# Grouped attentions without a rough pass: scores kept in an SBUF ring, half-group maxima folded from them and added later

## The reference

```python
# 4 batches; 16 query heads, 4 key heads, head width 128; layer 1 also turns q and k by rotary tables
q = rms_norm(heads(x @ Wq), q_norm_w)
k = rms_norm(heads(kv_in @ Wk), k_norm_w)      # layer 1: kv_in = context and x, 1857 rows; layer 3: context, 1601
scores = einsum('bqhd,bkhd->bhqk', q, repeat(k, 4)) / sqrt(128)
out = einsum('bhqk,bkhd->bqhd', softmax(scores), repeat(v, 4)) @ Wo
x = x + out
```

## Time and profile before

| what | us |
| --- | --- |
| median of three runs (3725.1 to 3730.5) | 3728.4 |
| profiled execution, first to last instruction (its span; its own time stands nowhere else) | 3724.8 |
| first block and groups of the first grouped attention | 476.0 to 541.3 to 1753.9 |
| first block and groups of the second | 2487.0 to 2533.9 to 3597.5 |

### The profile page before, as it was taken

The page is one execution under the profiler, slowest core; times in us unless marked ns, Lnnn a source line. Parts: engine busy times, 40 slices in busy tenths (PEclk is TensorE's granted clock), DMA queues, the critical chain, the costliest instruction groups (busy, mean ns, idle before and its releaser), DMA issues. The chain is left out here.

```text
span 3724.8 us, 63821 instructions
## 1 busy us (share of the span) xinstructions
PE 3484.8 (94%) x23912; PEld 2986.2 (80%) x23912; DVE 2317.7 (62%) x4551; ACT 2244.6 (60%) x5208; POOL 863.9 (23%) x1082
## 2 busy tenths in 40 slices
PE   6859969999999999998899999888999999999999
PEld 5659958888888889987666665677989899889888
DVE  8976767766776676664777776435554555545434
ACT  3327736676676676665466666325666666666653
POOL 0022134222322222221121120212322322223214
PEclk8879979999999999999999999898999999999999
DMA  5216521100010010001100000121010110100001
GB/s 183 89 66 217 181 80 39 57 15 24 15 56 24 18 54 15 18 12 47 61 1 37 37 1 1 74 93 32 21 53 26 39 41 26 53 21 18 7 29 41
DMA packets 59186, 179.04 MB, mean 48 GB/s; under 512 B 6084, under 2 KB 27776, under 8 KB 53888
## 3 DMA queue, kind: packets, MB, share of 16 engines
q1 hardware_dynamic: 53024, 135.57, 10.6%
q0 software_dynamic: 3696, 37.68, 2.7%
q10 hardware_dynamic: 2160, 1.71, 0.2%
HBM read 147.14 MB, written 24.13 MB: 46 GB/s over the span
## 5 line engine op out<-in xcount | busy, mean ns | idle before, releaser
L1140 PE MATMUL ps<-a_v_rows,a_probs 128*128 128x129 f32 (+1 forms) x7168 | 943.3, 276 | 0.5 <-DVE a_o_rows L1508 0.5
L1140 PEld LDWEIGHTS ps<-a_v_rows,a_probs 128*128 128x128 f32 (+1 forms) x7168 | 894.5, 191 | 41.1 <-issue 5.1
L1252 ACT ACTIVATE a_probs<-ps 128x512 f32<-128x512 f32 (+1 forms) x896 | 535.6, 598 | 606.0 <-PE ps L1129 604.8
L1483 DVE TENSOR_REDUCE a_neg<-ps 128x1 f32<-128x1024 f32 (+2 forms) x512 | 539.7, 1055 | 397.0 <-PE ps L1104 396.4
L1262 ACT ACTIVATE ps<-a_negb 128x512 f32<-128x512 f32 (+1 forms) x892 | 536.7, 602 | 58.3 <-DVE a_negb L1498 30.3
L1324 POOL TENSOR_SCALAR a_diag<-ident,a_negmax 128x128 fp32r<-128x128 f32 x256 | 157.1, 614 | 1466.1 <-DVE a_negmax L1491 1464.5
L1125 PE MATMUL ps<-a_qt,a_kt 128*128 128x512 f32 (+1 forms) x896 | 428.0, 478 | 1.4 <-PEq L72 1.4
L1031 PE MATMUL ps<-a_wr,a_ct 128*128 128x256 f32 (+1 forms) x2496 | 362.9, 287 | 19.0 <-DMA a_ct<-ctx_lo 16.9
L1031 PEld LDWEIGHTS ps<-a_wr,a_ct 128*128 128x128 f32 (+1 forms) x2496 | 336.4, 188 | 44.7 <-issue 15.7
L1129 PE MATMUL ps<-a_qt,a_kt 128*128 128x512 f32 (+1 forms) x896 | 354.9, 396 | 0.0
L1127 PE MATMUL ps<-a_qt,a_kt 128*128 128x512 f32 (+1 forms) x896 | 354.0, 395 | 0.0
(11 more groups left out here) (469 smaller groups left out, 5992.5 us busy)
## 6 DMA issues: line engine op xcount, KB each, us to landing
a_wf<-in_a_wq SPq DMA_DIRECT2D x32, 512.0 KB, 3.6
a_wf<-in_a_wo SPq DMA_DIRECT2D x32, 512.0 KB, 3.6
a_ct<-ctx_hi SPq DMA_DIRECT2D x8, 1090.0 KB, 7.9
a_ct<-ctx_lo SPq DMA_DIRECT2D x8, 1090.0 KB, 10.2
f_we<-in_f_experts SPq DMA_DIRECT2D x8, 1088.0 KB, 8.8
a_wf<-in_a_wkv SPq DMA_DIRECT2D x32, 256.0 KB, 2.7
ctx_hi<-a_ct SPq DMA_DIRECT2D x4, 1602.0 KB, 5.4
ctx_lo<-a_ct SPq DMA_DIRECT2D x4, 1602.0 KB, 9.3
```

Source lines behind the costliest of these rows:

```text
L1140: ins = pe.matmul(m.ps[:, 6 + i // 2, (i % 2) * 256:(i % 2) * 256 + VW], probs[0:r, n % 3, i * P:(i + 1) * P], v_rows[g % 2][0:r, t, :], s ...
L1252: act.activation(probs[0:r, n % 3, :], m.ps[0:r, 4 + n % 2, :], ACT.Exp)\
L1483: ins = dve.tensor_reduce(neg2[:, j, r % 2:r % 2 + 1], flat2(m.ps[:, rough_at(task):rough_at(task) + 2, :])[:, 0:e - a0], AX.X, ALU.max, n ...
```

## The change

The rough pass is gone (R in all its parts, with L1104, L1483, L1491, L1324), and the seeds are gone. Now:

- `scores` start their own accumulation, in four banks (0, 1, 4, 5) instead of two.
- ACT copies each score tile from PSUM to a slot of an SBUF ring (`keep`; 20 slots in a1, 18 in a3), where before it seeded.
- DVE folds it into the half-group's running maximum `peak` (`highest`; 128x512, one operand in SBUF, one in PSUM; none for a half's first tile).
- After a half's last tile, task MX: PE transposes `peak` (4 matmuls), DVE reduces to `negmax`, POOL makes four diagonals at once; then NB as before, one turn later.
- POOL adds `negb` to each ring slot (`shift`), KT + 2 turns after the scores. In a3 every fourth tile is added by DVE, and so is every second tile of the very last half in both.
- ACT takes the exponential in the slot, KT + 3 turns after the scores, and PE's `values` read the slot in that same turn. The list of turns is one group longer, for what still runs after the last scores.
- One key and one query buffer: the next group's are written behind the scores that last read them. One weight buffer `wf` in place of three. x is read and updated where it is kept (`m.x`); XC and the DMAs of x are gone.

The core of the diff:

```diff
-        "R8 GA14", "R9 RA6 GA15", "R10 RA7 RA8", "XC0 RA9 R11", "RS0 R12", "R13", "R14", "R15 W0 NX0", "NB0", "",
+        "MX1 RA3", "NB1 Q0 RA4", "Q1 RA5", "QN0 RA6", "W1 OX0 RA7 PR0 GP4", "KV0 RA8 QN1 GP5", "KV1 RA9 PX0 GA4 GP6",
...
+    SHIFT_LAG, EXP_LAG, VALUE_LAG = KT + 2, KT + 3, KT + 3
+    RING = VALUE_LAG + 2
+    SCORE_BANKS = (0, 1, 4, 5)
...
+        def by_vector(n):
+            u, t = divmod(n, KT)
+            if u == UNITS - 1:
+                return t % 2 == 1
+            return not rope and t % 4 == 3
...
 PE
+                    def MX(g, i):
+                        out = begin(("MX", g, i))
+                        pe.wait_ge(peaked, peaks(KT * (unit_of(g, i) + 1) - 1))
+                        for j in range(JG):
+                            ins = pe.transpose(out[:, j * P:(j + 1) * P], peak[:, j * P:(j + 1) * P], m.ident[:, :])
+                        ins.then_inc(item_ready, 1)
...
                     def scores(n):
-                        if n >= 2:
-                            pe.wait_ge(seeded, n - 1)
-                        out = m.ps[0:r, 4 + n % 2, :]
+                        if n >= 4:
+                            if (n - 4) % KT:
+                                pe.wait_ge(peaked, peaks(n - 4))
+                            else:
+                                pe.wait_ge(kept, n - 3)
+                        out = m.ps[0:r, SCORE_BANKS[n % 4], :]
...
 ACT
+                        act.activation(slot(n)[0:r, :], m.ps[0:r, SCORE_BANKS[n % 4], :], ACT.Copy).then_inc(kept, 1)
...
+                        act.wait_ge(shifted_dve if by_turn[n] else shifted, shifts[by_turn[n]][n])
+                        act.activation(slot(n)[0:r, :], slot(n)[0:r, :], ACT.Exp).then_inc(exp_done, 1)
...
 POOL
+                    def MX(g, i):
+                        u = unit_of(g, i)
+                        pool.wait_ge(item_free, number[("MX", g, i)] + 1)
+                        pool.tensor_tensor(diag[:, :, :], m.ident[:, :].unsqueeze(1).to_broadcast([P, JG, P]),
+                                           negmax[:, u % 2, :].unsqueeze(2).to_broadcast([P, JG, P]), ALU.mult)\
                             .then_inc(diag_done, 1)
+                    def shift(n):
+                        u, t = divmod(n, KT)
+                        r = tiles[t][1]
+                        if t == 0:
+                            pool.wait_ge(item_free, number[spread(u)] + 1)
+                        pool.wait_ge(kept, n + 1)
+                        pool.tensor_tensor(slot(n)[0:r, :], slot(n)[0:r, :], negb[0:r, u % 2, :], ALU.add)\
+                            .then_inc(shifted, 1)
...
 DVE
+                    def highest(n):
+                        dve.wait_ge(kept, n + 1)
+                        dve.tensor_tensor(peak[0:r, :], (slot(n - 1) if t == 1 else peak)[0:r, :],
+                                          m.ps[0:r, SCORE_BANKS[n % 4], :], ALU.max).then_inc(peaked, 1)
+                    def MX(g, i):
+                        src = begin(("MX", g, i)).rearrange("p (j n) -> p j n", j=JG)
+                        dve.tensor_reduce(negmax[:, unit_of(g, i) % 2, :].unsqueeze(2), src, AX.X, ALU.max, negate=True)\
+                           .then_inc(item_free, 1)
```

More of the change, by code:

```diff
@@ L762, in wanted @@
         return i == 2 or g + 2 < GROUPS
-    if (kind, i) == ("NB", 1) or (kind == "R" and i < 8):
-        return True
     return g + 1 < GROUPS
@@ L770, in plan_groups @@
     turns = []
-    for g in range(GROUPS):
+    for g in range(GROUPS + 1):
         for names in GROUP_TURNS[rope]:
@@ L1279, in _ @@
                                 does[task](g, i)
[L1280 to L1282 removed]
+                        if attend and n == END_AT:
+                            end_high(0)
+                    if attend:
+                        end_high(1)
                 @block.gpsimd
@@ new lines, in shift, with outputs @@
+                    def shift(n):
+                        u, t = divmod(n, KT)
+                        r = tiles[t][1]
+                        dve.wait_ge(item_free, number[spread(u)] + 1)
+                        dve.wait_ge(kept, n + 1)
+                        dve.tensor_tensor(slot(n)[0:r, :], slot(n)[0:r, :], negb[0:r, u % 2, :], ALU.add)\
+                           .then_inc(shifted_dve, 1)
+                    def outputs(u):
+                        dve.wait_ge(pv_done, KT * (u + 1))
+                        G = u % NG
```

393 lines of the change are left out of this document (177 added, 216 removed), and 13 rows, old and new, of tables (FIRST_TASKS, GROUP_TURNS).

## The result

The changed kernel takes 3826.97 us (median of 4 runs, 3823.57 to 3832.22), the kernel before 3728.19 (4 runs beside it): a ratio of 1.0264, 95% interval 1.0249 to 1.0278. The forecast was 3629 us, with 0.85 on faster. The error is 198 us, and its sign is wrong.

The account below looks back on a forecast made before the run. PE's instruction stream was taken as the bound; -40.6 us in the first attention and -59.0 in the second, together -99.6 against the 3728.4 us median, gave 3629 us. The range ran from 3540 to 3712.

Parts of the forecast that it names:

- Removed and added work on PE: Both attentions: rough matmuls out, -105.4 and -91.8 us; first blocks -12 and -11; transposes of folded maxima +13.8 each.
- unchanged, and it hides below PE: ACT, first attention's groups: a copy out of PSUM replaces the seed, both 0.60 us; load stays 51.4 against PE's 69.4.
- Below 1.04 nothing would be gained, since POOL is not the bound: POOL, first attention's groups: adds at 1.04 us give 48.6 us per group against PE's 69.4; cheaper adds gain nothing.
- if PE idles ... values for exponentials: Sign of being wrong: PE idle before scores or values for exponentials would mean ACT or POOL is the bound; no size.
- The clock, taken at 1.00: PE in both group windows: granted clock of 1.00 (2.4 GHz), read from the profile before.
- NB0 waits 3 us in the first attention, +48: PE's spread at one half-group: DVE reaches the transposed maxima 3.7 us late, so the spread waits 3: 16 x 3 = 48.
- The hold of POOL's operations on DVE: First attention, 14 products and sums with two SBUF inputs last longer under POOL operations: 0.35 us each on average, 4.9 us.
- The add at 1.04 us: POOL's add of a score tile, priced by the median of its 128x512 multiply; 1.59 us at most kept for the range.
- Start and tail, +2 per attention: End of each attention: 16.4 us from last scores' start, before 2.1; 14.6 of values skipped in first turns; net +2.
- POOL becomes the bound: Rival, slower: POOL's 30 adds per group at 1.59 us each, ACT's exponentials waiting on them; sum 3749 us, chance 0.11.
- 85 us for waits at the half-groups: PE's waits before the spread: 48 and 9 us in the first attention, 28 in the second.

Follow-up runs that it names:

- e13: e9 with POOL's add on 64 of a tile's 512 columns (output not the reference's): 3645.2 us, ratio 0.9782 to the kernel before.
- e6: Changed kernel with each add of a score tile asked for one half turn earlier (SHIFT_LAG KT + 1): 3757.0 us, ratio 1.0076 to the kernel before.
- e1: Changed kernel with weight split W0 asked for four half turns later in the first attention, two in the second: 3789.8 us.
- e9: Changed kernel with add one half turn earlier, weight split W0 later, DVE's close of item 0 later and its statistics behind the loop: 3702.6 us.
- e10: e6 with POOL's add on 64 of a tile's 512 columns (output not the reference's): 3694.2 us, ratio 0.9919 to the kernel before.
- e3: Changed kernel with the add's second operand repeated from 4 numbers a partition (output not the reference's): 3807.4 us.
- e8: Changed kernel with DVE's close of item 0 two turns later, its statistics behind the loop, PE's end_products(0) at END_AT + 4: 3814.8 us.

## Why the prediction was wrong, step by step

- **Removed and added work on PE: right as far as seen.** The first blocks are shorter by 11.5 us each (58.7 to 47.1 from VectorE's first weight split in the first, 47.2 to 35.7 from the first weight transfer's issue in the second), forecast 12 and 11. Folds 0.69 as said. With the four losses out, 3645 stands against 3629; but in e13 PE is still idle 63 and 40 us up to the last scores, so this near hit is no proof of the prices.
- **"unchanged, and it hides below PE" (ACT), and "Below 1.04 nothing would be gained, since POOL is not the bound": this is the step that failed.** I compared each engine's work per group with PE's and priced one chain, at the half-groups. I did not follow the new chain of every tile, POOL's add, ACT's exp, PE's values, with one turn of lead and ACT in order. Its waits stood in the sum at nothing. They cost 70 us for the late adds (e6) and 37 for the weights (e1); PE's waits for exps are 141.6 us in the changed kernel. The diff showed that W0 had come within two turns of W2 on one buffer; I gave it no price. That the queues matter was in my own list of what would prove me wrong ("if PE idles ... values for exponentials"), yet with no time.
- **The clock, taken at 1.00: wrong by the same step.** The waits bring 1.2 GHz for 75 us of the group stretches, where it was 15. At most half of the added 60 is lost, an estimate of up to 30 us. They are part of the prices of the four causes and no fifth one.
- **NB0 waits 3 us in the first attention, +48: wrong in place.** PE waits for the diagonal 24.3 us in the first attention's groups, where 57 were forecast, and 14.1 in the second's, where 28 were; 40.6 over all 64 half-groups. DVE's lateness does exist, but surfaces one to two turns earlier, where PE needs the bank of a key item (1.1 us at turn 14).
- **The hold of POOL's operations on DVE: right in kind, undersized.** I charged 4.9 us to one stretch of turns; in both attentions together the full adds cost 57 (e13 against e9) to 63 us (e10 against e6), of which ACT's wait for POOL is little (16.7 to 9.0 and 11.6 to 7.3 us). DVE's busy time in the two group stretches falls from 919 and 619 us in e9 to 802 and 586 in e13, with the same instructions. The key products' means of 1.05 and 1.11 us lie at the top of the range forecast, the sums' (0.47 and 0.85) below it. The Trainium skill, SBUF — State Buffer, section SBUF: two separate sides, names exactly this exclusion; its trace evidence here is L1440 at 1109 ns beside full adds and 674 beside those on 64 columns.
- **The add at 1.04 us: wrong, 1.26 at least and 1.42 in the mean;** the repeated operand of the earlier trace rows hid it, and by e3 its price alone was worth 20 us. The Trainium skill, GPSIMD Engine Reference, section 3.1 Elementwise — side-by-side cycle accounting, counts 2.6 cycles an element for an add with two inputs. By that figure, at the 1.2 GHz that the section gives, an estimate is 512 x 2.6 / 1.2 GHz = 1.11 us without what each instruction costs besides. The trace, with 1257 ns at the least, lies above the estimate, and the estimate above the 1.04 that I took. I had used that page's advice and not its figure.
- **Start and tail, +2 per attention: undersized.** The last values end 33.5 and 30.7 us after the last scores begin, where 16.4 was forecast; 12 us of it in all was the close of item 0 (e8), and with e9 it is 25.3 and 23.6. The rest of the excess was not taken apart further. The prediction's own terms, 16.4 - 2.1 - 14.6, give no +2 either but nothing.
- **The rivals.** "POOL becomes the bound" had the right sign by luck, and it had the place, the adds on which ACT's exps wait. Its mechanism is not what happened: POOL is idle a quarter of the first attention's groups and more of the second's, and e6 gained 70 us with POOL's work unchanged.

Four causes, with what each run gave back: lead of the adds 70, hold on VectorE 57, W0 37, close of item 0 12. Together 176 of 198; 16 us are left above the forecast, and the other 6 lie within what the sets of runs differ by. That so few are left is luck in good part: the forecast held 85 us for waits at the half-groups, of which 40.6 came (34.5 in e13), and two losses it did not hold are still in e13. One is W0 in the second attention's three groups with the keys' transfers (turn 25 takes 7.0 us there, 2.2 elsewhere: 14 us). The other: in three groups of the first attention ACT's sine tables now delay values. From e6, group 7:

```profile
1091.93 1.28 ACT L1277 ACT_TABLE_LOAD   x1
...
1093.22 1.90 ACT L1277 ACTIVATE a_cs<-a_cs 128x960 f32<-128x960 f32 x2
...
1095.13 1.28 ACT L1272 ACT_TABLE_LOAD   x1
```

4.5 us in ACT's order, and PE's values then wait 3.48; turn 8 is 4.8 us longer in groups 3, 7 and 11 (e13), again 14 us. No run moved either, so both are read, not tested.

## What to carry to other kernels

When a pass is replaced by work in a chain, compare not only each engine's load with the bound's, but each new link's lead with the longest thing that stands ahead of it in its own in-order queue: here one constant (the add one turn earlier) was worth 70 us, and a table entry that follows another on a single buffer 37. Price an operation by a row with the same kinds of operands, repeated or full, and count what a GpSimd operation with SBUF inputs takes from VectorE's two-input ones: here 57 to 63 us, nearly as much as its own lateness. A bound from averages says what a change can give; only the order of the queues says what it gives.
